# A Mamba block and two local-attention layers on one core: the first two elements and the last one get code of their own, and the hand-written order is split in three

## What is computed

```python
xz = x @ in_proj_w; xb, z = split(xz)
xb = silu(causal_depthwise_conv(xb, conv_w, conv_b))          # 4 taps, 256 channels
proj = xb @ x_proj_w
dt = softplus(proj[..., :8] @ dt_proj_w + dt_proj_b)
b, c = proj[..., 8:24], proj[..., 24:]
def step(state, ts):                                          # over 512 tokens
    da = exp(dt_t[:, :, None] * a)                            # 256 channels x 16 states
    state = da * state + dt_t[:, :, None] * b_t[:, None, :] * u_t[:, :, None]
    return state, einsum('bds,bs->bd', state, c_t)
y = (scan(step) + D_param * xb) * silu(z) @ out_proj_w
# then, two layers, 8 heads of 64, windows of 64 tokens that look at one window before:
h = shift_token(x); q, k, v = split(h @ wqkv)
q, k = rotary_xpos(l2norm(q) * qs, l2norm(k) * ksc)
x = x + softmax(mask(8 * q @ k.T)) @ v @ wo
h = layernorm(shift_token(x)); a, g = split(h @ w1 + b1)
x = x + (a * gelu(g)) @ w2 + b2
```

## Time and profile before

| | us |
|---|---|
| median of 3 runs | 2429.0 (2427.78 to 2432.51) |
| the profiled execution | 2435.31 |
| its span, first to last instruction | 2433.5 |
| busy PE / DVE / ACT / POOL | 1903.3 / 1883.9 / 1767.4 / 1715.1 |
| first scan starts / last scan of element 0 ends | 55.4 / 134.8 |
| last scan of element 15 ends | 2193.9 |

### The profile page before, as it was taken

The page is one execution under the profiler, slowest core; times in us unless marked ns, Lnnn a source line. Parts: engine busy times, 40 slices in busy tenths (PEclk is TensorE's granted clock), DMA queues, the critical chain, the costliest instruction groups (busy, mean ns, idle before and its releaser), DMA issues.

```text
span 2433.5 us, 43992 instructions
## 1 busy us (share of the span) xinstructions
PE 1903.3 (78%) x15823; PEld 1130.5 (46%) x15936; DVE 1883.9 (77%) x3461; ACT 1767.4 (73%) x3955; POOL 1715.1 (70%) x1572
## 2 busy tenths in 40 slices
PE   2246789796978879697878979698887979788866
PEld 0013455363635546363645536364544636364634
DVE  3557797979878797988879797987879798887442
ACT  2345778696978878696877869697887869686644
POOL 1969595977959596886959597795959688693110
PEclk7566999899999999998999989999999989999988
DMA  5444343535445343634535363544535263540100
GB/s 171 122 121 116 102 121 98 144 93 132 108 118 132 93 125 81 151 89 127 136 95 121 96 143 93 135 105 118 131 97 127 78 158 88 138 112 20 26 20 9
DMA packets 126345, 261.08 MB, mean 107 GB/s; under 512 B 26928, under 2 KB 59696, under 8 KB 125872
## 3 DMA queue, kind: packets, MB, share of 16 engines
q1 hardware_dynamic: 126128, 258.27, 40.9%
HBM read 185.42 MB, written 42.99 MB: 94 GB/s over the span
## 4 chain that ended last, share of the span: by engine, by line
PE 30%; POOL 24%; DVE 21%; ACT 13%; issue 8%; DMA 3%; SPq 1%; POOLq 0%; DVEq 0%; ACTq 0%
POOL dbu L662 9%; POOL gy L679 9%; DVE hs L634 4%; POOL kr L996 4%; PE b_bank L358 3%; PE f_bank L358 3%; DVE m L927 3%; ACT late L892 3%; DVE kr L941 2%; PE y_sum L585 2%; PE b_bank L719 2%; DMA spread<-steps 2%; DVE ss L914 2%; PE b_bank L745 2%; PE f_bank L1027 2%
## 5 line engine op out<-in xcount | busy, mean ns | idle before, releaser
L634 DVE TENSOR_TENSOR_SCAN hs<-da,dbu 128x512 f32<-128x512 f32 x512 | 623.2, 1217 | 101.4 <-POOL dbu L662 68.9
L662 POOL TENSOR_TENSOR dbu<-spread,bc 128x512 f32<-128x512 f32 x512 | 653.6, 1277 | 27.5 <-DMA spread<-steps 27.4
L679 POOL TENSOR_TENSOR gy<-hs,bc 128x512 f32<-128x512 f32 x512 | 652.7, 1275 | 22.4 <-DVE hs L634 10.6
L610 ACT ACTIVATE da<-spread,rest 128x512 f32<-128x512 f32 x512 | 364.3, 712 | 160.1 <-DVE hs L634 130.6
L996 POOL TENSOR_TENSOR kr<-kr,rn 128x512 f32<-128x512 f32 x256 | 264.5, 1045 | 23.3 <-ACT rn L850 13.2
L719 PE MATMUL b_bank<-rest,h_t 128*128 128x512 f32 x384 | 232.7, 716 | 60.3 <-DVE kr L941 56.3
L719 PE MATMUL f_bank<-rest,h_t 128*128 128x512 f32 x384 | 217.9, 666 | 25.9 <-DVE kr L941 17.9
L585 PE MATMUL y_sum<-gy,rest 128*32 128x512 f32 x1024 | 147.2, 650 | 101.0 <-POOL gy L679 101.0
L358 PE MATMUL b_bank<-first,kr 128*128 128x128 f32 x768 | 128.0, 292 | 109.1 <-DVE kr L941 90.5
L358 PE MATMUL f_bank<-first,kr 128*128 128x128 f32 x768 | 126.5, 291 | 72.8 <-DVE kr L941 65.4
L358 PEld LDWEIGHTS b_bank<-first,kr 128*128 128x128 f32 x768 | 89.3, 147 | 191.9 <-DVE kr L941 145.8
(11 more groups left out here) (172 smaller groups left out, 4884.6 us busy)
## 6 DMA issues: line engine op xcount, KB each, us to landing
spread<-steps SPq DMA_DIRECT2D x256, 512.0 KB, 5.2
vs<-v SPq DMA_DIRECT2D x96, 260.0 KB, 6.9
steps<-k_t SPq DMA_DIRECT2D x32, 512.0 KB, 3.3
bc<-bc_rows SPq DMA_DIRECT2D x32, 512.0 KB, 6.3
gate<-gates SPq DMA_DIRECT2D x32, 512.0 KB, 6.3
gates<-kr SPq DMA_DIRECT2D x16, 512.0 KB, 2.7
gates<-late SPq DMA_DIRECT2D x16, 512.0 KB, 3.4
vs<-v SPq DMA_DIRECT2D x32, 130.0 KB, 5.5
```

The source lines that it names most:

```text
L610: e.activation(da[:, :], spread[:, slot(b, s // 2), 0, :], ACT.Exp, scale=a_neg[:, s:s + 1]).then_inc(decayed.sem, 1)
L634: e.tensor_tensor_scan(hs[:, s % 2, :], da[:, :], dbu[:, s % 2, :], 0.0, ALU.mult, ALU.add).then_inc(scanned.sem, 1)
L662: e.tensor_tensor(dbu[:, s % 2, :], spread[:, slot(b, s // 2), 1, :], bc[:, s % 2, :], ALU.mult).then_inc(fed.sem, 1)
L679: e.tensor_tensor(gy[:, s % 8, :], hs[:, s % 2, :], bc[:, 2 + s % 2, :], ALU.mult).then_inc(read_out.sem, 1)
```

## The change

1. Entry of element 0: its products go to six banks instead of one (`entry_bank`), so that PE no longer waits for ACT and DVE between them; dt and dt*u of element 0 are made by DVE instead of POOL.
2. Scan of elements 0 and 1: the decay alternates between two banks (`da`, `lb[0]`), and DVE makes 21 of 32 products `gy` of element 0 and 11 of 32 of element 1, each issued right behind the next scan.
3. B of element 15 (`wide`): its takes go through all eight banks, rotated q tiles have tiles of their own (in `bc`), squares go to `gy`, pairs of heads alternate between two pairs of banks (two pairs are scored ahead), values between two banks, and the turned outputs have banks of their own.
4. `ORDER` has three words per engine: one for the first rounds, one that is repeated 11 times, one for the last rounds. The repeated word has the same steps as before in a partly different order. On SP, per round: the stores of u and b, c come before the store of x1; the store of x1 and the four loads of L1156 come between the store of dt and that of dt*u, and the v window copies come some steps earlier.

```diff
-def weave(word, late, **chains):
...
+def weave(first, usual, last, **chains):
+    for word in (first, *[usual] * ROUNDS, last):
         for part in word.split():
             for _ in range(int(part[1:])):
...
+                next(chains[part[0]])
...
+        def entry_bank(b, part):
+            if b:
+                return e_bank
+            return dict(turn=e_bank, i0=fa[0], i1=fa[1], i2=fa[2], i3=lb[0], x=lb[1], d0=fa[0], d1=fa[1])[part]
...
                 E.wait_ge(*dt_size(b, h))
+                e.tensor_scalar(dt[:, h, :], entry_bank(b, f"d{h}")[:, :], dt_b[:, h:h + 1], 0.0, ALU.add, ALU.max).then_inc(dt_clipped.sem, 1)
+                if b == 0 and h == NH2 - 1:
+                    for _ in step_inputs(E, e, 0):
+                        pass
...
+        SHARED = 2
+        def by_dve(b, s):
+            return b < SHARED and (s % 3 > 0, s % 3 == 1,)[b]
...
+        def read_product(E, e, b, s):
+            E.wait_ge(*c_loaded(b))
+            E.wait_ge(*scanned(b, s))
+            if s > 7:
+                E.wait_ge(*summed_up(b, 2 * (s // 8 - 1) + s % 2))
+            elif b > 0:
+                E.wait_ge(*x1_made(b - 1))
+            e.tensor_tensor(gy[:, s % 8, :], hs[:, s % 2, :], bc[:, 2 + s % 2, :], ALU.mult).then_inc(
+                (read_out if b >= SHARED else dve_read if by_dve(b, s) else pool_read).sem, 1)
...
+        def decay(b, s):
+            return lb[0] if b < 2 and s % 2 else da
...
             for s in range(NSCAN):
+                if s > 1 and by_dve(b, s - 2):
+                    E.wait_ge(*reads(b, s - 2)[-1])
                 E.wait_ge(*decayed(b, s))
                 E.wait_ge(*fed(b, s))
+                e.tensor_tensor_scan(hs[:, s % 2, :], decay(b, s)[:, :], dbu[:, s % 2, :], 0.0, ALU.mult,
                                      ALU.add).then_inc(scanned.sem, 1)
+                if s and by_dve(b, s - 1):
+                    read_product(E, e, b, s - 1)
...
+            def bank_list(self, b):
+                if self is wb and b == B - 1:
+                    return [*lb, da, y_sum, *fa]
+                return self.banks
...
+            def head_banks(self, b):
+                L = self.bank_list(b)
+                if len(L) == 3:
+                    return [L[0:2]] * 4, [L[2]] * 8
+                return [L[0:2], L[3:5]] * 2, [L[2], L[5]] * 4
...
+            if wide:
+                score(1)
+                yield
+                for g in range(HEADS // 2):
+                    for hd in (2 * g, 2 * g + 1):
+                        turn(hd)
+                        yield
+                    for hd in (2 * g, 2 * g + 1):
+                        value(hd)
+                        yield
+                    if g < 2:
+                        score(g + 2)
+                        yield
+                    else:
+                        turn_out(g - 2)
+                        yield
```

The repeated word of SP before and after (a letter is a stream, so S is u, z, b and c stores, F the dt stores, E the input, M the state's loads):

```diff
-        "M1 S1 M1 S2 F2 M7 B1 M2 E1 C1 M1 B1 M1 A1 M1 A1 M3 B1 M5",
+        "M1 S3 F1 M1 B1 F1 M6 B1 M2 B1 A1 M2 E1 M1 C1 M1 A1 M8",
```

More of the change, by code:

```diff
@@ L94, in use_table @@
             self.e.preload_act_table_set(name)
-def weave(word, late, **chains):
-    late = {part[0]: int(part[1:]) for part in late.split()}
-    while chains:
+def weave(first, usual, last, **chains):
+    for word in (first, *[usual] * ROUNDS, last):
         for part in word.split():
             for _ in range(int(part[1:])):
[L103 to L106, removed]
+                next(chains[part[0]])
+    for chain in chains.values():
+        for _ in chain:
+            raise AssertionError("a step is left over")
 def build(nc, a, out):
@@ L412, in dve_enter @@
             for h in range(NH2):
+                bank = entry_bank(b, f"i{h}")
                 E.wait_ge(*pad_zeroed(b))
@@ L437, in pool_steps @@
                 yield
+        def pool_steps(E, e, b):
+            if b:
+                yield from step_inputs(E, e, b)
+            else:
+                for _ in range(2 * NH2):
+                    yield
         def pe_enter(E, e, b):
@@ L509, in act_steps, with reads @@
             yield
+        SHARED = 2
+        def by_dve(b, s):
+            return b < SHARED and (s % 3 > 0, s % 3 == 1,)[b]
+        def reads(b, s):
+            if b >= SHARED:
+                return [read_out(b - SHARED, s)]
+            n = [0, 0]
+            for other in range(b + 1):
+                for step in range(s + 1 if other == b else NSCAN):
+                    n[by_dve(other, step)] += 1
+            return [sem(k - 1) for sem, k in ((pool_read, n[0]), (dve_read, n[1])) if k]
+        def read_product(E, e, b, s):
[7 more added lines that the diff above has]
+                (read_out if b >= SHARED else dve_read if by_dve(b, s) else pool_read).sem, 1)
         def group_rows(b, g):
@@ L543, in sp_state @@
             if b > 0:
-                E.wait_ge(*read_out(b - 1, NSCAN - 1))
+                for done in reads(b - 1, NSCAN - 1):
+                    E.wait_ge(*done)
             load_bc(1, c_loaded)
@@ L582, in pe_state @@
                     E.wait_ge(*skipped(b - 1, 1))
-                E.wait_ge(*read_out(b, 8 * (m // 2) + 6 + k))
+                for done in reads(b, 8 * (m // 2) + 6 + k):
+                    E.wait_ge(*done)
                 for j in range(4):
@@ L606, in act_state @@
                 E.wait_ge(*loaded(b, s // 2))
-                if s:
+                if s and decay(b, s) is decay(b, s - 1):
                     E.wait_ge(*scanned(b, s - 1))
+                elif s > 1:
+                    E.wait_ge(*scanned(b, s - 2))
                 E.use_table(EXP_LN)
-                e.activation(da[:, :], spread[:, slot(b, s // 2), 0, :], ACT.Exp,
+                e.activation(decay(b, s)[:, :], spread[:, slot(b, s // 2), 0, :], ACT.Exp,
                              scale=a_neg[:, s:s + 1]).then_inc(decayed.sem, 1)
@@ L704, in pe_attention @@
         def pe_attention(E, e, b, w, l, x, f):
+            L = w.bank_list(b)
+            wide = len(L) > 3
             for n, take in enumerate(TAKES):
-                kind, t, bank = take[0], int(take[1]), w.banks[(n + 1) % 3]
-                if n > 2:
-                    E.wait_ge(*w.freed(b, TAKES[n - 3]))
-                elif b > 0:
+                kind, t, bank = take[0], int(take[1]), L[(n + 1) % len(L)]
+                if n >= len(L):
+                    E.wait_ge(*w.freed(b, TAKES[n - len(L)]))
+                elif b > 0 and bank in w.banks:
                     E.wait_ge(*(f.added(b - 1) if bank is f.sum else f.gated(b - 1, 2)))
@@ L713, in pe_attention @@
                     E.wait_ge(*dt_clipped(b + 2, 1))
+                if bank is lb[0] and n == 2 and b == 0:
+                    E.wait_ge(*scanned(1, NSCAN - 1))
                 if kind == "x":
@@ L880, in act_attention, with weigh @@
                     yield
-            X = w.banks[0:2]
-            for hd in range(HEADS):
+            XS, _ = w.head_banks(b)
+            def weigh(hd):
+                X = XS[hd // 2]
                 E.wait_ge(*w.peaked(b, hd))
@@ L968, in share @@
                 yield
+            if len(L) > 3:
+                for hd in range(2):
+                    peak(hd)
+                    yield
             for hd in range(0, HEADS, 2):
-                peak(hd)
-                yield
-                peak(hd + 1)
-                yield
+                for other in range(hd, hd + 2) if len(L) == 3 else range(hd + 2, min(hd + 4, HEADS)):
+                    peak(other)
+                    yield
                 if hd:
@@ L994, in normalise @@
                     E.wait_ge(*w.added(b, n))
-                x = heads(w.rotated_tile(take))
+                x = heads(w.rotated_tile(b, take))
                 e.tensor_tensor(x, x, w.rn[:, n, :].unsqueeze(2).to_broadcast([P, HEADS, DH]),
```

141 lines of the change are left out of this document (80 added, 61 removed), and 80 rows, old and new, of the table ORDER.

## The result

The changed kernel takes 2449.48 us, median of 5 runs (2445.9 to 2457.26), beside 2432.32 for the kernel before in 5 runs: a ratio of 1.0077, 95% interval 1.0058 to 1.0096. It is slower, by some 17 us; forecast was 2389. The profiled execution has a span of 2447.7 us, against 2433.5.

The account below looks back on a forecast made before the run. Middle rounds were held bound by hand-over order, no engine full; the first scans by POOL, the end by a chain of waits. Terms -10 - 9 - 3 + 0 - 5 - 7 - 6 = -40 took 2429.0 to 2389 us; range 2362 to 2411.

Parts of the forecast that it names:

- the repeated word: Order of the middle rounds: same steps, neighbours exchanged, taken as 0 us; bounds +9 and -11 for 11 rounds.
- The slower rival: SP's queue in the 11 repeated rounds: residual loads before the dt*u store cost 4.5 us a round, 2439 us; chance 0.03.
- Entry: Entry of element 0: a bank per product brings the first scan near 45 us, -10 us; bounds -6 and -12.
- Scan 0: Scan of element 0: POOL and DVE products share one line, 2.2 us a step, -9 us; bounds -23 and 0.
- scan 1: Scan of element 1: eleven products move from POOL to DVE, -3 us; between -13 and +3.
- rival 1: Scans 0 and 1: POOL and DVE do not hinder each other in long products, 24 us more, 2365 us; chance 0.13.
- What the earlier start is worth: From scan 1 to the end: the start's 22 us gain arrives without loss; bounds -4 and +10.
- Rival 2: First elements' lead is lost: start gives 10 rather than 22 us, end 14 rather than 18; 2405 us; chance 0.22.
- Rival 3: Middle rounds: the repeated word is better by 1 us a round or more, 12 in all; 2377 us; chance 0.20.
- A of 15 beside B of 14: Near the end: an order made for this 119.0 us stretch regains some idle time, -5 us; between 0 and -12.
- Rotation: B of 15, projections and rotation: with eight banks DVE sets the pace, 33 us instead of 40.0, -7; between -3 and -10.
- heads: B of 15, heads and output projection: next pair scored ahead, 27.7 us instead of 34.0, -6; between -2 and -9.

Follow-up runs that it names:

- e2: The changed kernel with only SP's queue back in its old order in the middle rounds; 2410.75 us.
- e1: The changed kernel with all engines and SP back in the order of before in the middle rounds; 2387.1 us.
- e3: The changed kernel with only PE, ACT, DVE and POOL back in their old orders in the middle rounds, SP's kept new; 2430.1 us.
- e4: The changed kernel with DVE's statistics of the next element's input one scan later in the middle rounds; 2404.53 us (one execution).
- e5: The changed kernel with the next element's input load put before the v window copies and both spread loads in SP's repeated order; 2445.33 us.
- e9: The changed kernel with SP's repeated order altered: input and a spread load before B's window copies, the other spread load before A's; 2404.5 us.
- e11: e1 with the entry of element 0 in one bank again, dt and dt*u staying on DVE; 2399.57 us.
- e10: e1 with all 32 products gy of element 0 on DVE, none on POOL; 2383.66 us.
- e6: e1 with all products gy of elements 0 and 1 made by POOL again, the second decay bank kept; 2406.87 us.
- e7: e1 with the last element's second layer in three banks and the old tiles again, with its old order of head pairs; 2401.5 us.
- e12: e10 with 21 instead of 11 of the 32 products of element 1 on DVE; 2383.77 us.

## Why the prediction was wrong

**The step that failed** is the repeated word: "Same steps, neighbours exchanged: ... Taken as 0", with +9 as its upper bound. It costs 5.5 us a round, 66 us in twelve. Of that the engines' exchanges, which the paragraph names and takes as nothing, cost 1.7 a round by themselves (e2 less e1), and SP's 3.3 (e3 less e1). On SP the paragraph prices one exchange, the loads between the dt stores, and passes over another that the diff shows and my own description of the change names: the v window copies come some steps earlier. I looked at SP's queue at the right cost, an issue of 0.36 to 0.6 us each, and not at what stands behind it: who needs the load that is now last, and how long it takes to land behind four copies and two spread loads (8.4 us instead of 3.0). In the trace of before the statistics started at 1300.55 and the input, issued at 1295.93, took 3.2, so the slack was 1.4 us, and the next scan stood behind the statistics on DVE. That could have been read before the run. (e4, e5 and e9 show it.)

The slower rival (0.03) had the queue and a price near the measured one, 4.5 a round and 2439, but the wrong exchange: with the residual loads where the change puts them, e9 makes a round of 140.1. The stretch between the last scan and the next first one, where it would have shown, did not grow (43.0 us, before 43.4). That its price came near was luck. It deserved more than 0.03: it was the only term with a factor of 11.

**Entry: -10, measured -12.5** (first scan), just beyond the bound of -12, and -12.5 by the medians of e11 and e1; the runs that share this entry have their first scan at 41.6 to 44.5. The chain up to dt*u was right: |dt| is done at 26.4 instead of 28.3, because the four input products took 6.6 us and not 8.3, and dt*u at 31.9. Behind it, the end of the tables (41.7) was not what the first scan (42.9) waited for. It waited for POOL's first `dbu`, which ran beside the tables and took twice its 1.26 us:

```profile
40.27 2.55 POOL L800 TENSOR_TENSOR dbu<-spread,bc 128x512 f32<-128x512 f32 x1 [32.98 <-DMA spread<-steps]
```

The prediction had named this, "tables hindered by POOL's first inputs", as a bound; it came the other way round, POOL hindered by the tables.

**Scan 0: -9, measured -10.5; scan 1: -3, measured -6.6.** That a DVE instruction with two SBUF inputs waits for POOL's running one holds; the prediction lacked the other side. In scan 0 the same scan releases DVE's product and POOL's next operation, the product starts some 0.2 us ahead, and POOL is held. In scan 1 DVE has other work between, most products start inside an operation of POOL, and DVE is held. Both in the changed kernel, first a pair of scan 0, then one of scan 1:

```profile
82.06 0.67 DVE L634 TENSOR_TENSOR gy<-hs,bc 128x512 f32<-128x512 f32 x1
82.23 1.62 POOL L634 TENSOR_TENSOR gy<-hs,bc 128x512 f32<-128x512 f32 x1 [0.74 <-DVE hs L768]
...
198.84 1.27 POOL L800 TENSOR_TENSOR dbu<-spread,bc 128x512 f32<-128x512 f32 x1
199.10 1.56 DVE L634 TENSOR_TENSOR gy<-hs,bc 128x512 f32<-128x512 f32 x1
200.07 1.72 POOL L634 TENSOR_TENSOR gy<-hs,bc 128x512 f32<-128x512 f32 x1
```

Of the 20 products traced in scan 0 two last longer than 0.70 us (0.86 and 1.06); of the ten traced in scan 1 eight last 0.75 to 1.56, with a mean of 1.10 over the ten. The Trainium skill ("SBUF — State Buffer", section "Who interferes with whom") says of the ports shared for such a pair that "Issue order, not op shape, decides who blocks": these rows agree, with one order in scan 0 and the other in scan 1. That a product costs POOL 0.29 in the mean and not its whole 0.67 is because only part of it lies beside POOL's operation: in e10 0.44 to 0.50 us in 28 of 30 traced cases, and POOL's operation is then 0.30 to 0.37 longer. With 0.29 a product, POOL's line in scan 0 is 32 + 11 operations of 1.27 and 21 x 0.29, 60.7 us (measured busy: 60.18), and not the 67.0 I had; the other 8 us of the 68.9 are hand-overs, which my 2.2 a step happened to cover: there the size was luck. The independent case (rival 1, 2365) is refuted by the stretched operations of both engines. In scan 1 I allowed 11 waits of up to 1.22 us for DVE; the ten traced products were 4.3 us longer together.

**What the earlier start is worth:** kept but for 2 us. The lead is 31.2 us at the end of scan 1 and 29.2 at x1 of 2, and e1, e6 and e11 show that it reaches the end. Rival 2 falls. Rival 3 (a better word) had the wrong sign.

**A of 15 beside B of 14: -5, measured -4.8. Rotation -7 and heads -6: measured -7.9 and -7.6** with the cut at the first maximum (42.6 and 32.1 before), and e7 confirms both. From the second pair of heads on, the exponentials of the pairs start 5.1 us apart, against the 5.4 I drew up, and behind its first tile DVE waits three times for ACT in the rotation, 2.9 us together, against the 3 I allowed.

Without the repeated word the sum would have been near: e1 has exactly that, and it gains 46 by the medians and 41.3 by the spans, where I had 40. In part that is luck. By the spans the start gives 26.1 up to x1 of 2 (I had 22) and the end 21.7 (18), and the rounds between take 6.5 back, of which 4.2 lie in the round where e1 crosses from one order to the other.

## What to carry to other kernels

Where an order is repeated, a neighbour exchanged costs its price times the rounds; go through the exchanges of the DMA queue one by one, and ask of each which transfer now stands last and which in-order engine waits for it, with the scan or product behind the waiting instruction. An issue of half a microsecond says nothing of it: four copies and two spread loads in front more than doubled the time to landing. Where the queue cannot be changed, the other end can: with DVE's waiting step moved one scan later, most of the loss went too (e4). And test a change with several parts by taking one part back: here the part that was meant as mere reordering gave back more than all the others brought, and a change at one place of one word turns 2449 into 2404. The lowest medians measured are those of e10 and e12, 2384 us, not clearly apart from e1's 2387.

## What the runs showed of the hardware

- A load's time to landing depends on what was issued in front of it on SP's queue: for the input of a middle round 2.9 to 3.2 us with nothing just in front (before), 7.3 to 9.4 behind four window copies and two spread loads (changed kernel). The Trainium skill has the rule ("DMA: Bandwidth & Descriptors", section "Queues, rings and completion order"): each DMA engine takes a ring's descriptors in ring order. The runs agree: put the input in front and it lands in 3.4, and the spread loads are the late ones.
- DVE and POOL hold each other when both read two inputs from SBUF, and the later one waits. Where the DVE product starts some 0.2 us ahead, it keeps its 0.67 us and POOL's operation of 1.27 takes 1.56 (mean of 31, e10). Where it starts inside POOL's operation, it lasts up to 1.56 us (scan 1 of the changed kernel). In the kernel before, the four-element L339 of rows 5 on `mr_x` takes 0.15 to 0.16 us in the three of 16 cases in which POOL is idle, and 0.91 to 1.27 in the 13 in which POOL is at work.
- The granted clock of a middle round is 0.92 in the changed kernel, 0.98 before and 0.96 in e9 (mean over about one round each); PE's busy time for the same round is 119.3, 114.4 and 116.9 us. A share below 1.0 is a mix of the level of 2.4 GHz and that of 1.2. How much of the 5.5 us is the clock, and how much the wait itself, the runs do not separate.
